# Moving one VectorE sum ahead of another in the last layer of a gated graph network

## The reference

```
for l in range(4):
    m   = x @ weight[l]
    agg = segment_sum(m[src], dst)
    gi  = agg @ w_ih.T + b_ih ;  gh = x @ w_hh.T + b_hh
    r = sigmoid(i_r + h_r) ; z = sigmoid(i_z + h_z) ; n = tanh(i_n + r * h_n)
    x = (1 - z) * n + z * x
out = layernorm(x0 + (x + x0))          # x0: the input; no scale, no shift
```

## Time and profile before

| what | value |
|---|---|
| median of 3 runs | 2382.85 us (2382.22 to 2384.59) |
| the profiled execution, its own time | 2379.24 us |
| its span, first to last instruction | 2377.3 us |
| TensorE clock granted, mean | 0.981 |
| PE busy | 2251.5 us, 95% |
| DVE busy | 2185.7 us, 92% |
| ACT busy | 1846.3 us, 78% |
| POOL busy | 1747.0 us, 73% |

### The profile page before, as it was taken

How to read it: one execution, slowest core, us unless ns; L and a number is a source line. 1 busy time by engine, 2 the same in 40 slices (tenths; PEclk the granted TensorE clock), 3 DMA queues, 4 the chain that set the end, 5 groups by cost and what they waited for, 6 DMA issues and landing times.

```text
span 2377.3 us, 49608 instructions
## 1 busy us (share of the span) xinstructions
PE 2251.5 (95%) x11728; PEld 1904.3 (80%) x11728; DVE 2185.7 (92%) x4408; ACT 1846.3 (78%) x3483; POOL 1747.0 (73%) x1654
## 2 busy tenths in 40 slices
PE   3899999999989999999979999999989999999996
PEld 2788888888868888888868888888877877777885
DVE  7699999999869999999959999999969999999998
ACT  1588888888758888888847888888856888888887
POOL 3778888888477777777647777777747888888884
PEclk7899999999999999999989999999999999999998
DMA  2355555555535555555535555555543555555553
GB/s 57 98 154 161 160 157 159 159 161 157 151 110 167 171 167 170 171 172 169 170 100 168 172 171 167 172 166 172 171 140 101 155 155 159 153 152 156 157 156 116
DMA packets 277063, 362.44 MB, mean 152 GB/s; under 512 B 107754, under 2 KB 186586, under 8 KB 276980
## 3 DMA queue, kind: packets, MB, share of 16 engines
q1 hardware_dynamic: 238196, 309.20, 42.5%
q0 software_dynamic: 38784, 52.30, 9.6%
HBM read 208.71 MB, written 179.20 MB: 163 GB/s over the span
## 4 chain that ended last, share of the span: by engine, by line
PE 65%; DVE 18%; issue 10%; ACT 4%; another core or an unknown queue 1%; DMA 1%; DVEq 1%; ACTq 0%; POOL 0%; SPq 0%; POOLq 0%
PE pR L839 17%; PE pZ L839 17%; PE pHN L839 8%; PE pA L827 8%; PE pO L906 6%; PE pIN L839 4%; PE pA L839 4%; DVE bn L1405 3%; DVE aggT L1344 2%; DVE diff L1374 2%; DVE y_rows L1398 2%; DVE diff L1380 2%; PE pH L778 2%; DVE narg L1370 1%
## 5 line engine op out<-in xcount | busy, mean ns | idle before, releaser
L675 POOL DMA_INDIRECT gath<-state,idx x900 | 933.3, 1037 | 266.4 <-issue 255.6
L652 POOL TENSOR_TENSOR h_lo<-hT,h_hi 128x500 fp32r<-128x500 f32 (+1 forms) x400 | 376.1, 940 | 220.7 <-ACT h_hi L1025 115.0
L675 POOL DMA_INDIRECT gath<-in_x_dram,idx x300 | 347.5, 1158 | 102.3 <-issue 74.8
L1055 ACT ACTIVATE rg<-pR,bsum 128x500 f32<-128x500 f32 x400 | 269.7, 674 | 132.5 <-PE pR L839 61.2
L1363 DVE SCALAR_TENSOR_TENSOR narg<-pHN,bhh,rg 128x500 f32<-128x500 f32 x400 | 294.0, 735 | 62.9 <-ACT rg L1055 31.1
L1380 DVE TENSOR_TENSOR diff<-pZ,diff 128x500 f32<-128x500 f32 x400 | 269.0, 672 | 9.6 <-ACT pZ L1063 6.7
L1344 DVE TENSOR_TENSOR aggT<-pA,hT 128x500 f32<-128x500 f32 x396 | 265.8, 671 | 8.5 <-remote 4.9
L1335 DVE TENSOR_TENSOR a_lo<-aggT,a_hi 128x500 fp32r<-128x500 f32 x396 | 271.2, 685 | 0.8
L1037 ACT CAST sel<-sel 128x504 fp32r (+1 forms) x400 | 245.6, 615 | 30.2 <-DVE flag_i L1319 29.8
L1063 ACT ACTIVATE pZ<-pZ,bsum 128x500 f32<-128x500 f32 x400 | 256.3, 641 | 10.6 <-remote 10.4
L906 PEld LDWEIGHTS pO<-ident,newT 128*125 128x125 f32 x1400 | 202.5, 187 | 55.0 <-DVE newT L1389 16.4
(11 more groups left out here) (205 smaller groups left out, 6404.0 us busy)
## 6 DMA issues: line engine op xcount, KB each, us to landing
columns<-newT SPq DMA_DIRECT2D x300, 250.0 KB
hT<-columns SPq DMA_DIRECT2D x300, 250.0 KB
state<-o_rows SPq DMA_DIRECT2D x300, 224.0 KB
x_rows<-in_x_dram SPq DMA_DIRECT2D x200, 224.0 KB
out_dram<-o_rows SPq DMA_DIRECT2D x91, 224.0 KB
gath<-state,idx POOLq DMA_INDIRECT x900
state<-o_rows SPq DMA_DIRECT2D x300, 26.0 KB
idx<-edge_src SPq DMA_DIRECT2D x395, 1.5 KB
```

Of the source, the lines that this page charges most:

```text
L652: nc.gpsimd.tensor_tensor(part_of(h_lo, u)[:, cols], hT[:, u % RING, cols], part_of(h_hi, u)[:, cols].bitcast(F32), ALU.subtract).then_inc ...
L675: pool.indirect_dma_start(out=gath[:, u % RING, j, :], out_offset=None, in_=states[l], in_offset=bass.IndirectOffsetOnAxis(ap=idx[:, u % R ...
L1055: nc.scalar.activation(rg[:, :], pR[:, 0:COLS], ACT.Sigmoid, bias=bsum[:, 0:1]).then_inc(s_r, 1)
```

## The change

In every step of the last layer from the fifth on, DVE does `residual` of block b-2 directly behind `n_argument`, then `aggregate` of block b+2, then `row_stats` of block b-2. Before, `aggregate` came first. (`remainder` calls `residual`; `added` is true in the last layer alone, so the other three layers are as they were. Steps 98 and 99 have no `aggregate`.)

```diff
                         summed = after(i, u, 1 if ramp else 2)[:2] if exists(i, u, 2) else None
+                        if added and not ramp:
+                            remainder(*after(i, u, -ROWLAG))
                         if summed and not (ramp and u == 3):
                             aggregate(l, *summed)
                         if added and not ramp:
-                            remainder(*after(i, u, -ROWLAG))
                             row_stats(*after(i, u, -ROWLAG)[:2])
                         if half:
                             moments(*half, RING * (half[1] + 1))
```

## The result

The changed kernel takes 2428.77 us in the median (5 runs, 2424.99 to 2432.24) against 2383.42 us for the kernel before (5 runs, 2382.22 to 2385.74): a ratio of 1.0179, 95% interval 1.0166 to 1.0193. The two medians are 45 us apart, a quotient of 1.0190; the measurement's own estimate of the ratio, 1.0179, is +43 us on 2382.85. The forecast was +42. Both 2428.77 and the interval's ends, taken on the 2382.85 us of before (2422.4 to 2428.8), lie in the range 2417 to 2433.

The account below looks back on a forecast made before the run. The last layer was taken as bound twice, by DVE and by a DVE-ACT ring of 5.69 us. 71 x 0.58 + 18 x 0.08 less 0.6 for early steps made +42.0 us: forecast 2424.9 us, range 2417 to 2433.

Parts of the forecast that it names:

- the ring: Last layer, DVE and ACT: a closed chain of waits that takes just the plain step's 5.69 us.
- Effect 1: On DVE, `residual` ahead of `aggregate` makes a_hi on ACT later; the ring grows by 0.58 us (0.56 to 0.60).
- Effect 2: On DVE, `row_stats` no longer follows its own producer: 0.12 us less a step, counting only where DVE alone decides.
- Early steps: Last layer, steps 4 to 8, without normalisation: DVE decides, -0.6 us for the five steps.
- the full ring: The ring with normalisation in it, steps 9 to 97 of the last layer: 89 steps, +42.6 us.
- Effect 4: What else waits for the later `aggregate` (`low_part`, `product`, edge sums): all covered by at least 0.6 us, no cost.
- the signs: Trace marks named beforehand: later a_hi, new ACT and DVE idle time, 6.27 us plain steps, longer z product wait on PE.
- A: Rival: DVE stays the last layer's bound, only its shorter wait counts; -11.3 us, 2371.6 us; 7%.
- B: Rival: ACT absorbs the delay and DVE's shorter wait gives nothing; no change within 0.2%, 2383 us; 3%.
- C: Rival: slower but less, part of the delay won back on ACT; if half, +21 us, 2404 us; 6%.
- D: Rival: PE idles about 1 us a step and its granted clock falls at times; +44 us on top, 2469 us; 4%.
- the bound of 0.71: Upper bound in us for `residual`'s place on DVE, today's start to start with the wait; gives +52.7 us, held unlikely.

Follow-up runs that it names:

- e1: Changed kernel with ACT's last-layer order turned to n gate, z gate, a_hi, sel (a_hi stood ahead of the z gate): 2377.6 us, ratio 0.9993.
- e2: Kernel before, plus one spare copy on ACT between z gate and sel in each last-layer step from step 4: 2415.92 us, ratio 1.016.
- e3: Kernel before, plus the same spare copy as e2 but ahead of the normalisation's first half, in ACT's idle time: 2379.09 us, ratio 1.0005.
- e4: Kernel before, `aggregate` still first, with the row statistics moved behind `difference` on DVE: 2379.99 us, ratio 1.0.
- e5: Kernel before, with the normalisation's second half on ACT moved ahead of the n gate: 2376.55 us, ratio 0.9987.
- e6: Changed kernel, with the normalisation's second half on ACT moved ahead of the n gate as in e5: 2386.5 us, ratio 1.0034.
- e9: Changed kernel with sel widened early, ahead of the normalisation's first half, and a same-size spare copy in its old place on ACT: 2421.52 us, ratio 1.0186.
- e8: Changed kernel with `row_stats` as well as `residual` ahead of `aggregate`: 2501.92 us, ratio 1.0509.
- e7: Kernel before with the edits of both e4 and e5: 2378.59 us, ratio 0.9998.
- e10: e6 with h_lo on POOL moved behind the gathers in steps with b mod 5 = 4, from step 9: 2423.76 us, ratio 1.0192.
- e11: e7 with h_lo on POOL moved behind the gathers in steps with b mod 5 = 4, from step 9: 2412.82 us, ratio 1.014.
- e12: Changed kernel with only h_lo on POOL moved behind the gathers in steps with b mod 5 = 4, from step 9: 2437.71 us, ratio 1.0241.

## Why the prediction was right

- The step on which it rested, that the last layer is bound twice and the ring over `n_argument`, `aggregate`, a_hi, z gate, sel, normalisation, r gate and `r_times_hn` has no reserve, was right: e1 takes the loss away, e2 makes the like of it without touching DVE, e3 shows that ACT's idle time is elsewhere.
- Effect 1, the growth of the ring: `aggregate` starts 1.18 us behind `n_argument` (1.18 forecast), a_hi 1.88 (1.88 to 1.92), the plain step takes 6.27 (6.27), with a shift 6.36 (6.37), with moments 6.27 (6.27).
- Effect 2, the wait for the result of the instruction just ahead: `row_stats` starts 0.59 us behind its neighbour and not 0.71. It buys nothing while the ring decides (e4), and 0.12 us a step once it doesn't (e5 against e6). The Trainium skill's sentence that the semaphore costs nothing extra (VectorE: DVE Perf Modes, section "The DRAIN you can't avoid") does not hold here for a wait on the instruction just ahead: 0.71 us from start to start with it, 0.59 without it.
- Early steps: four of the five went from 5.65 or 5.66 to 5.52 to 5.54 us, as forecast. The fifth, step 7, has moments, which the forecast left out of account; it took 7.72 us in place of 6.96, since its first instruction of `moments` ran beside h_lo and lasted 1.85 us (below), so that the five together gained nothing (-0.6 forecast, +0.3 measured).
- Two steps at the ends of the full ring also came out otherwise than in the sum: step 9, with the collision before and after, went from 6.82 to 6.93 us (+0.58 forecast), and step 97, in which ACT has no sel left to widen, from 6.18 to 6.06, DVE's own work (+0.08 forecast). Together with the early steps, steps 4 to 97 grew by 41.8 + 0.3 = 42.1 us against 42.0 forecast. The size of a step was right to 0.01 us; that the total is right to 0.1 is in part luck, as these misses cancel.
- Effect 4 missed a reader: the edge sums on PE wait for sel, which stands behind a_hi. e9 shows that it did no harm. One of the signs was wrong too: PE's wait at the z product did not grow, it shrank (weight loads of pZ: 23.2 us in 56 waits before, 3.4 in 12 after). PE now waits in other places. Waits of PE in the changed kernel, 1900 to 2300 us:

```profile
PEld pO L906 <- issue: 23.0, 32, 0.8
PEld pH L906 <- issue: 17.4, 26, 0.8
...
PEld pZ L839 <- issue: 3.4, 12, 0.3
```

The transposes wait for the new state, which comes behind the late `r_times_hn`. PE is idle for 20.9 of 400 us after and for 9.2 before; where it waits says nothing of the bound.

- Of the rivals, A and B fall with the time itself and C with the steps of 6.27 us; e2 and e8 show besides that DVE alone is not the bound. D is refuted by the granted clock of 1.00. Its working was off: it said that PE would idle about 1 us a step, though its own 5.61 of 6.27 us leave 0.66, and 89% busy; measured are 0.33 us and 95% (539 of 570 us). PE's busy time is no fixed sum, since the ends of matmuls are modelled. e8 shows that there was room even so: PE is busy for 83% of the last layer there (473 of 570 us) and the clock stayed at 1.00.
- The range does not follow from its terms. They give 2382.85 + 40.5 - 2 = 2421 as the lower end, where 2417 stands without a reason, and the upper end of 2433 leaves out the bound of 0.71. The result lies inside either way.
- The +3 us between the medians' +45 and the forecast's +42 are not in the steps that changed, as far as the profiled executions tell, in which these grew by 42.1 us. The other layers scatter by more than that.

## What to carry to other kernels

An engine that is busy for 99% of a stretch need not be the only bound: look whether any instruction on it starts a hand-over (here 0.11 us) behind another engine's result in every step, and then follow that ring through both engines' orders. In an in-order queue, idle time can take up work that stands ahead of it, between the last instruction that the ring needs and the wait itself, and nothing that stands behind it: 0.50 us of work a step cost nothing on one side of ACT's n gate and 38 us on the other. A reorder that gives its own engine a shorter wait must be priced by what it makes late for the others, and to cash it in, the ring has to be loosened as well. A shorter step also moves the engines against each other, and the gain can be lost to a collision that had been rare before.

## What the runs showed of the hardware that was not expected

- A VectorE `tensor_tensor` with both inputs in SBUF (a_lo, 0.67 us) that meets a GpSimd `tensor_tensor` on SBUF (h_lo, 1.27 us) takes up to 1.85 us and ends 0.54 us after it, which is about its own time from start to start. From step 14 on it was long in all 17 steps with a shift in e6 and in e7. In the changed kernel and in the kernel before, from step 9 on, it was long in step 9 alone; in 17 later steps of the kernel before h_lo ends 0.01 to 0.07 us behind a_lo's start, and a_lo keeps its 0.67 to 0.68. In step 7 of the changed kernel an instruction of `moments` with both inputs in SBUF, of 0.19 us by its neighbours, took 1.85 and ended within 0.1 us of h_lo's end, though h_lo is recorded as starting 0.52 us behind it. VectorE instructions with one input in PSUM overlapped h_lo in dozens of steps and kept their length (`aggregate` 0.665 us over h_lo, 0.670 otherwise, in e6). The Trainium skill (SBUF — State Buffer, section "SBUF: two separate sides") says that such a pair competes for one exclusive lock, that the one that starts first holds it for its whole instruction, and that the other is blocked for that time. The lengths and ends of these runs agree. The recorded order does not always: in e6 h_lo is recorded 0.04 us behind a_lo's start, and yet a_lo is the one that waits. Starts on GpSimd are rough, so this doesn't decide against the lock.
- A pause of PE of 2.9 us in e10 was followed by slower matmuls: the four transposes behind it took 1.21 us (0.60 in the step before), and the mean granted clock in the stretch was 0.59 of 2.4 GHz, between the two levels of 2.4 and 1.2 GHz and so at the lower one for most of it. Busy time by stretch in e10, ahead of the pause and behind it:

```profile
2048.00:2057.00 9.00, 8.93 (x45) 7.24 (x45) 7.71 (x18) 6.26 (x13) 7.29 (x7) 1.00 0.58 156
2060.00:2064.00 4.00, 3.63 (x12) 3.19 (x13) 4.00 (x11) 3.22 (x7) 3.24 (x4) 0.59 0.28 83
```

The shorter waits of PE in the changed kernel (0.8 us at most from 1900 to 2300 us) left it at 1.00.
- A wait of the r gate, of up to 3.2 us in e10, 3.4 in e11 and 2.0 in e12, for which the profile names no releaser inside the core, as told above.
